# A cross-attention block in split fp32r: x in three buffers, and work of the first steps and of every fourth step in another order or on another engine

## The reference

```python
scale = HEAD_DIM ** (-0.5)
h = _layernorm(x, gamma, beta)                       # over the last axis of 256
Q = (h @ Wq).reshape(B, NQ, N_HEADS, HEAD_DIM)
K = (context @ Wk).reshape(B, NC, N_HEADS, HEAD_DIM)
V = (context @ Wv).reshape(B, NC, N_HEADS, HEAD_DIM)
attn = jnp.einsum('bihd,bjhd->bhij', Q, K)
attn = jax.nn.softmax(attn, axis=-1) * scale
vals = jnp.einsum('bhij,bjhd->bihd', attn, V).reshape(B, NQ, INNER)
out = vals @ Wo + bo
return x + out
```

## Time and profile before

| | us |
|---|---|
| runs | 339.98 (median), 339.65, 396.95 |
| the profiled execution | 339.38 |
| its span | 337.3 |
| mean granted TensorE clock | 0.995 of full speed |

### The profile page before, as it was taken

How to read it: one execution, slowest core, us unless ns; L and a number is a source line. 1 busy time by engine, 2 the same in 40 slices (tenths; PEclk the granted TensorE clock), 3 DMA queues, 4 the chain that set the end, 5 groups by cost and what they waited for, 6 DMA issues and landing times.

```text
span 337.3 us, 9748 instructions
## 1 busy us (share of the span) xinstructions
PE 322.7 (96%) x3773; PEld 283.2 (84%) x3773; DVE 258.4 (77%) x585; ACT 254.7 (76%) x799; POOL 161.3 (48%) x294
## 2 busy tenths in 40 slices
PE   5999997999999999999999999999999999999986
PEld 4868777888889988888998888899888889988864
DVE  4898855787887788787877878877887878668764
ACT  4898883888778877787677887778777876777872
POOL 4688954463563364631563435633646315333330
PEclk9999997999999999999999999999999999999999
DMA  6860001020000200002000200002000010001000
GB/s 182 258 186 2 1 26 32 2 82 7 2 3 2 87 0 3 2 2 87 1 3 2 81 10 2 0 3 88 2 2 0 2 34 2 2 0 34 2 3 31
DMA packets 10764, 10.70 MB, mean 32 GB/s; under 512 B 960, under 2 KB 10176, under 8 KB 10720
## 3 DMA queue, kind: packets, MB, share of 16 engines
q1 hardware_dynamic: 10192, 9.64, 9.3%
q10 hardware_dynamic: 416, 0.33, 0.3%
q0 software_dynamic: 112, 0.13, 0.2%
HBM read 8.00 MB, written 2.10 MB: 30 GB/s over the span
## 4 chain that ended last, share of the span: by engine, by line
PE 78%; ACT 9%; DVE 6%; POOL 4%; issue 1%; DMA 1%; DVEq 0%; SPq 0%; POOLq 0%; ACTq 0%
PE mix_ps L866 15%; PE ring_ps L837 12%; PE ring_ps L932 11%; PE o_ps L957 10%; PE ring_ps L890 9%; PE ring_ps L989 8%; PE ring_ps L1023 6%; ACT prob L475 4%; DVE prob L689 2%; PE ring_ps L1030 2%; ACT qk_hi L485 2%; PE ring_ps L910 1%; PE o_ps L798 1%; POOL prob L383 1%; POOL wo_lo L322 1%
## 5 line engine op out<-in xcount | busy, mean ns | idle before, releaser
L383 POOL TENSOR_SCALAR prob<-prob,inv 128x256 f32<-128x256 f32 x192 | 90.3, 488 | 121.7 <-DVE inv L681 121.7
L475 ACT ACTIVATE prob<-ring_ps,neg_max 128x256 f32<-128x256 f32 x256 | 118.3, 474 | 21.7 <-DVE neg_max L674 21.7
L674 DVE TENSOR_REDUCE neg_max<-ring_ps 128x2 f32<-128x512 f32 x128 | 81.3, 677 | 1.0 <-PE ring_ps L837 0.8
L866 PE MATMUL mix_ps<-prob_t,v_sb 128*64 128x256 f32 x504 | 61.5, 385 | 0.5 <-DVE prob_t L779 0.5
L779 DVE COPY prob_t<-ring_ps 128x512 f32<-128x512 f32 x64 | 41.9, 687 | 21.6 <-PE ring_ps L989 20.3
L699 DVE TENSOR_TENSOR qk_lo<-ring_ps,qk_hi 128x512 fp32r<-128x512 f32 x64 | 44.1, 689 | 15.6 <-ACT qk_hi L485 15.6
L475 ACT ACTIVATION_READ_ACCUMULATOR prob<-ring_ps,neg_max 128x1 f32 x256 | 52.8, 206 | 0.0
L485 ACT ACTIVATE qk_hi<-ring_ps 128x512 fp32r<-128x512 f32 x64 | 38.7, 605 | 14.1 <-PE ring_ps L932 14.1
L866 PEld LDWEIGHTS mix_ps<-prob_t,v_sb 128*64 128x64 f32 x504 | 33.4, 136 | 18.3 <-issue 0.6
L989 PE MATMUL ring_ps<-ident,prob 64*128 64x64 f32 x1024 | 38.6, 223 | 1.8 <-DVE prob L689 1.1
L837 PE MATMUL ring_ps<-qk_hi 64*128 64x256 f32 x256 | 39.9, 301 | 0.3 <-DVE qk_lo L699 0.3
(11 more groups left out here) (116 smaller groups left out, 697.0 us busy)
## 6 DMA issues: line engine op xcount, KB each, us to landing
x_in<-in_x_dram SPq DMA_DIRECT2D x8, 256.0 KB, 2.9
out_dram<-y_sb SPq DMA_DIRECT2D x7, 256.0 KB, 2.2
c_in<-in_ctx_dram SPq DMA_DIRECT2D x7, 192.0 KB, 2.8
w_raw<-in_L_xattn_Wq_dram SPq DMA_DIRECT2D x8, 128.0 KB, 3.4
w_raw<-in_L_xattn_Wo_dram SPq DMA_DIRECT2D x4, 256.0 KB, 6.3
w_raw<-in_L_xattn_Wk_dram SPq DMA_DIRECT2D x4, 128.0 KB, 3.8
w_raw<-in_L_xattn_Wk_dram SPq DMA_DIRECT2D x8, 64.0 KB, 3.5
w_raw<-in_L_xattn_Wv_dram SPq DMA_DIRECT2D x2, 256.0 KB, 5.1
```

The costliest lines, as they stand in the source:

```text
L383: last = nc.gpsimd.tensor_scalar(prob[:, e, r, :], prob[:, e, r, :], inv[:, e, r:r + 1], SCALE, ALU.mult, ALU.mult)
L475: last = nc.scalar.activation(prob[:, e, r, :], score_bank(u, e)[:, r * ROWS:(r + 1) * ROWS], ACT.Exp, bias=neg_max[:, e, r:r + 1], accum_ ...
L674: nc.vector.tensor_reduce(neg_max[:, e, :], score_bank(u, e)[:, :].rearrange("p (r j) -> p r j", r=RT), AX, ALU.max, negate=True).then_inc ...
L866: last = nc.tensor.matmul(ps[h * HALF:(h + 1) * HALF, first:first + ROWS], v_sb[:, w // RT % 2, j, p * P + h * HALF:p * P + (h + 1) * HALF ...
```

## The change

- x_in has three buffers. x of sequence 2 is loaded with no wait, x of sequence b >= 3 after x_norm and x_bias of sequence b-3. SyncE's loop is written out step by step, and the load of bo moves from GpSimd's queue to the end of SyncE's weight loads.
- `bias(0)` moves from the end of step 2 to the end of step 4, ahead of `bias(1)`.
- Sequence 1's norm moves from GpSimd to VectorE, in step 1, one row tile on either side of `keys_lo(0)`. Its statistics move from the end of step 0 to places further up in step 0.
- The low part of weight piece 8 moves from VectorE (step 0) to GpSimd, ahead of step 0. GpSimd's `context_for_values(0)` goes: V of sequence 0 is made from c_t itself.
- h's high part moves from between `keys_lo(0)` and `keys_lo(1)` to behind `last_head` in the steps 2, 6, ..., 26. In step 2 weight pieces 20 and 21 stay ahead of `keys_lo(1)`.
- The first step's banks are taken in the same order as in all others, so that the second pair's scores of step 1 wait for one copy of each engine in place of two.

```diff
@@ the lists, buffers and banks
-    LO_VECTOR = (0, 4, 5, 8, 9, 13, 20, 21)
-    LO_POOL = (1, 2, 3, 6, 7, 10, 11, 12, 14, 15, 16, 17, 18, 19, 22, 23)
+    LO_VECTOR = (0, 4, 5, 9, 13, 20, 21)
+    LO_POOL = (1, 2, 3, 6, 7, 8, 10, 11, 12, 14, 15, 16, 17, 18, 19, 22, 23)
...
-        x_in = sb("x_in", [P, 2, RT, D])
+        x_in = sb("x_in", [P, X_BUFS, RT, D])
...
-            return ring[u % 3]
+            return ring[u % 3 if u else 2]
...
-            return ring[(u - (e // 2 if u else 1 - e // 2)) % 3][e % 2]
+            return ring[(u - e // 2) % 3][e % 2]
...
-        x_banks = ring[2]
+        x_banks = ring[0]
@@ SyncE
+            sp.dma_start(bo_b[:, :], b_o.partition_broadcast(P)).then_inc(bo_in, 16)
...
                 b = of_seq(u, LOAD, 2)
                 if b is not None:
-                    sequence, used = number(b + turns(2)), number(b - 1 + turns(2))
-
-                    sp.wait_ge(x_norm_ready, used)
-                    sp.wait_ge(x_bias_ready, used)
-                    load_x(b, sequence)
-                    sp.wait_ge(c_turned, used)
-                    load_c(b, sequence)
+                    if b >= X_BUFS:
+
+                        sp.wait_ge(x_norm_ready, b - X_BUFS + 1)
+                        sp.wait_ge(x_bias_ready, b - X_BUFS + 1)
+                    load_x(b)
+
+                    sp.wait_ge(c_turned, b - 1)
+                    load_c(b)
@@ GpSimd
             for n in (1, 2, 3, 6, 7):
                 weight_lo(n)
-            pool.dma_start(bo_b[:, :], b_o.partition_broadcast(P)).then_inc(bo_in, 16)
-            context_for_values(0)
+            weight_lo(8)
...
                     deviation(b)
-                    norm(b)
+                    if b >= 2:
+                        norm(b)
...
                 if u == 2:
                     weight_lo(22)
-                    pool.wait_ge(bo_in, 16)
-                    bias(0)
...
+                for b in (0, 1) if u == PER_SEQ else (of_seq(u, SPLIT_H, 2),):
+                    if b is not None:
+                        if b == 0:
+
+                            pool.wait_ge(bo_in, 16)
...
+                        pool.wait_ge(x_norm_ready, b + 1)
+                        bias(b)
@@ VectorE
                 if u == 0:
-                    weight_lo(8)
                     weight_lo(9)
+                    rows_statistics(1, 0)
...
+                if u == 1:
+
+                    dve.wait_ge(x_turned, 1)
+                    norm(1, (0,))
                 keys_lo(0)
+                if u == 0:
+                    rows_statistics(1, 1)
+                if u == 1:
+                    norm(1, (1,))
+                if u == 2:
+                    weight_lo(20)
+                    weight_lo(21)
...
                 if u < 2:
                     last_head()
+                keys_lo(1)
+                if u == 0:
+                    variance(1)
+                if measured is not None:
+                    deviation_base(measured)
+                if u >= 2:
+                    last_head()
                 b = of_seq(u, SPLIT_H, 1)
                 if b is not None:
...
                         nc.vector.tensor_copy(h_hi[:, b % 2, d, :], h_full[:, d, :])\
                             .then_inc(h_hi_ready, 1)
-                if u == 2:
-                    weight_lo(20)
-                    weight_lo(21)
-                keys_lo(1)
-                if measured is not None:
-                    deviation_base(measured)
-                if u >= 2:
-                    last_head()
...
-                        statistics(1)
+                        deviation_base(1)
                         weight_lo(13)
@@ TensorE
-                            pe.wait_ge(prob_t_ready[h], BATCH * (u - 1) + (2 if u == 1 else 1))
+                            pe.wait_ge(prob_t_ready[h], BATCH * (u - 1) + 1)
...
-                pe.wait_ge(c_val_ready, b + 1)
+
+                tiles = c_val if b else c_t
+                if b:
+                    pe.wait_ge(c_val_ready, b)
```

More of the change, by code:

```diff
@@ L33, in cross_attention_block @@
     STEPS = SEQS * PER_SEQ
-    LOOP_STEPS, LOOPS = 2 * PER_SEQ, 3
     LAST = STEPS + 2
@@ L61, in cross_attention_block @@
     FOR_O = {0: 15, 1: 20, 2: 23, 3: 24}
-    LO_VECTOR = (0, 4, 5, 8, 9, 13, 20, 21)
-    LO_POOL = (1, 2, 3, 6, 7, 10, 11, 12, 14, 15, 16, 17, 18, 19, 22, 23)
+    LO_VECTOR = (0, 4, 5, 9, 13, 20, 21)
+    LO_POOL = (1, 2, 3, 6, 7, 8, 10, 11, 12, 14, 15, 16, 17, 18, 19, 22, 23)
     WARM = 6
+    X_BUFS = 3
     SHIFT = 16
@@ L159, in cross_attention_block @@
         w_in = [sem(f"w_in{i}") for i in range(len(PIECES))]
-        x_loaded = [sem("x_loaded0"), sem("x_loaded1")]
+        x_loaded = [sem(f"x_loaded{k}") for k in range(X_BUFS)]
         c_loaded = [sem("c_loaded0"), sem("c_loaded1")]
@@ L212, in of_seq @@
             return b if rest == 0 and first <= b < SEQS else None
[L214 to L224, removed]
         def before(n, pieces):
@@ L242, in _ @@
         def _(sp):
-            def number(n):
-                return n if isinstance(n, int) else sp.snap(n)
             def load_weight(n):
@@ L264, in load_weight, with load_x, load_c, step @@
                                  rows.rearrange("(g p) n -> p g n", p=P)).then_inc(w_in[n], 16)
[L266 to L272, removed]
+            def load_x(b):
+                sp.dma_start(x_in[:, b % X_BUFS, :, :], x_v[b]).then_inc(x_loaded[b % X_BUFS], 16)
+            def load_c(b):
+                sp.dma_start(c_in[:, b % 2, :, :], c_v[b]).then_inc(c_loaded[b % 2], 16)
+            load_x(0)
             for n in range(0, 10):
                 load_weight(n)
-            load_x(1, 1)
-            load_c(1, 1)
+            load_x(1)
+            load_c(1)
             for n in range(10, len(PIECES)):
                 load_weight(n)
-            def step(u, turns):
+            sp.dma_start(bo_b[:, :], b_o.partition_broadcast(P)).then_inc(bo_in, 16)
+            def step(u):
                 b = of_seq(u, LOAD, 2)
                 if b is not None:
-                    sequence, used = number(b + turns(2)), number(b - 1 + turns(2))
-                    sp.wait_ge(x_norm_ready, used)
-                    sp.wait_ge(x_bias_ready, used)
-                    load_x(b, sequence)
-                    sp.wait_ge(c_turned, used)
-                    load_c(b, sequence)
+                    if b >= X_BUFS:
[4 more added lines that the diff above has]
+                    load_c(b)
                 b = of_seq(u, PUT)
@@ L296, in step @@
                 elif b is not None:
[L297 to L301, removed]
+                    sp.wait_ge(y_ready, b + 1)
+                    sp.dma_start(y_v[b], y_sb[:, b % 2, :, :]).then_inc(y_free[b % 2], 16)
+            for u in range(-1, LAST):
+                step(u)
             sp.wait_ge(y_free[0], 16 * (SEQS // 2 + 1))
@@ L335, in norm @@
                 for r in range(RT):
-                    last = nc.gpsimd.tensor_scalar(x_norm[:, r, :], x_in[:, b % 2, r, :],
+                    last = nc.gpsimd.tensor_scalar(x_norm[:, r, :], x_in[:, b % X_BUFS, r, :],
                                                    mean_var[:, r, 0:1], rstd[:, r:r + 1],
@@ L341, in context_for_values @@
             def context_for_values(b):
-                if b >= 2:
+                if b >= 3:
                     pool.wait_ge(v_made, PER_SEQ * (b - 1))
@@ L351, in bias @@
                 for r in range(RT):
-                    last = nc.gpsimd.tensor_tensor(x_bias[:, b % 2, r, :], x_in[:, b % 2, r, :],
+                    last = nc.gpsimd.tensor_tensor(x_bias[:, b % 2, r, :], x_in[:, b % X_BUFS, r, :],
                                                    bo_b[:, :], ALU.add)
@@ L396, in step @@
                     context_for_values(b)
-                b = of_seq(u, SPLIT_H, 1)
                 if u == 2:
                     weight_lo(22)
-                    pool.wait_ge(bo_in, 16)
-                    bias(0)
[L404 to L411, removed]
+                for b in (0, 1) if u == PER_SEQ else (of_seq(u, SPLIT_H, 2),):
+                    if b is not None:
+                        if b == 0:
+                            pool.wait_ge(bo_in, 16)
+                        if b >= 2:
+                            pool.wait_ge(y_ready, b - 1)
+                        pool.wait_ge(x_norm_ready, b + 1)
+                        bias(b)
             for u in range(-1, LAST):
-                step(u, lambda n: 0)
+                step(u)
         @block.scalar
@@ L597, in rows_statistics @@
             def rows_statistics(b, r):
-                k = b % 2
-                dve.wait_ge(x_loaded[k], 16 * (b // 2 + 1))
+                k = b % X_BUFS
+                dve.wait_ge(x_loaded[k], 16 * (b // X_BUFS + 1))
                 nc.vector.bn_stats(bn[:, r, :], x_in[:, k, r, :]).then_inc(stats_done, 1)
@@ L618, in statistics, with norm @@
                 deviation_base(b)
-            def norm(b):
```

(14 more changed lines are left out.)

## The result

The changed kernel takes 331.77 us, the median of four runs (331.59 to 332.07); the kernel before took 339.81 beside it. One of the four runs of the kernel before took 396.95 us and is left out of the ratio, which is 0.9767, 95% interval 0.9748 to 0.9786: faster by 2.3%. The forecast was 331.9 us. The profiled execution takes 332.07 us, 7.3 less than the profiled one before; its span is 330.1 us, 7.2 less.

A forecast was written before the change was run, and what follows sets the result against it. TensorE, busy for 322.7 of 337.3 us, bounds the kernel, so gains lie in its idle time and clock. 0.6 + 0.49 + 4.33 + 2.4 = 7.8 us off 339.38 gives 331.6, median about 331.9; range 329.8 to 335.2.

The forecast's parts named there:

- Part 1, the load of x: Step 3: sequence 2's x loads early, so VectorE's and TensorE's stalls and the low clock go; 4.33 us, bounds 2.6 to 4.43.
- Part 2, h's high part: Steps 6, 10, ..., 26: fourth head's scaling takes 0.62 us for 1.34 with GpSimd quiet; 0.40 us each, 2.4 in all.
- Part 3, steps 0 to 2: First steps: 0.6 us gained by step 2's start (bounds 0 and 1.05), and 0.49 us in step 2.
- the prediction's own sign: Start of step 2: its scores by 31.2 us in place of 31.8 if the forecast is right.
- step 0's gain would not be lost ahead of step 1's maxima: Step 1: as the statistics leave the place ahead of the maxima, step 0's gain of some 0.4 us is kept.
- the lower bound: End of step 1: turn's second half at 30.5 if norm waits for GpSimd's scalings and the fourth head for a low part.
- its alternative, a sum 0.3 us smaller: Step 1: by the skill's rule, the norm on VectorE contends with GpSimd's scaling, making the sum 0.3 us smaller.
- The norm rival: Steps 0 to 2: norm on VectorE and GpSimd's scalings block each other; nothing gained or up to 0.5 lost; chance 0.10.
- L1011 waited for nothing: Sign of a right forecast: L1011 with no wait for wv_lo.
- rivals on the fourth head: Steps 6, 10, ..., 26: the fourth head stays late; 2.4 us back, 334.3 us; chance 0.15.
- on the clock after the change: Step 3 keeps a wait or the clock still falls; price 1.7 us, 333.6 us; chance 0.12.
- on placement: All 32 steps: third buffer moves prob and others by 2,048 bytes a partition, slower access; 346 at 0.45 us a step; chance 0.03.

The follow-up runs named there:

- x_three_only: Kernel before with x in three buffers and nothing else, the load of bo and the bias staying where they were: 335.02 us, ratio 0.9881.
- low_part_waits_only: Kernel before, h's high part unmoved, but GpSimd's low part of h waits until VectorE has scaled the fourth head (steps 6, 10, ..., 26): 336.59 us.
- norm_on_gpsimd: Changed kernel with sequence 1's norm back on GpSimd, ahead of step 1's scaling: 331.50 us.
- step1_head_alone: Changed kernel, but in step 1 GpSimd starts low parts of pieces 15 to 18 only after VectorE scales the fourth head: 330.89 us, 330.62 us run again.

## Why the prediction was right, point by point

**Part 1, the load of x.** Forecast 4.33 us from step 3, measured 4.2 by the windows and 4.4 in the times of x_three_only alone (339.44 - 335.02). The cause was shown by that run. The clock's share was seen as fixed; it is a matter of the execution, 0 or some 1.7 us of the 4.3. Since 13 of 18 runs of the kernel before had it, the forecast from one profiled execution met the median; with one of the other five the same reading would have given 2.9 us (an estimate: step 3's 12.55 us in low_part_waits_only less 9.61). That is luck.

**Part 2, h's high part.** Forecast 0.40 us in each of six steps, 2.4 in all; measured 0.38 in the first, and 2.3 over the six. That the gain comes from GpSimd being late and not from VectorE's order was argued; low_part_waits_only showed it. The rule that the prediction took from the Trainium skill (SBUF — State Buffer, section "Who interferes with whom"), that such a VectorE instruction and a GpSimd one lock each other out for whole instructions, agrees: 1.34 and 0.62 us in step 6, and 1.39 and 0.61 us in step 1, for the same two instructions.

**Part 3, steps 0 to 2.** This is the term that was mis-sized: 1.09 us forecast (0.6 by step 2's start and 0.49 in step 2), 0.67 measured by the start of step 3. The 0.6 came to 0: the scores of step 2 start at 31.82 for 31.77, where the prediction's own sign asked for 31.2. It is a sum of two. Step 0 gave 0.61, more than the 0.4 forecast; step 1, which was to give 0.2, took 0.66 back.

Two steps of the reasoning failed. The first is that step 0's gain would not be lost ahead of step 1's maxima, as the statistics had left that place. The low part of piece 13 still stood there and waited 0.81 us for ScalarE, which was no earlier, and 0.19 us of the gain was left at the maxima. norm_on_gpsimd, with the norm where it was before, shows the same: its steps 0 and 1 together take 19.01 us (12.26 to 31.27) for 19.21 before (12.56 to 31.77), 0.2 us less. The second is the collision at the end of the step. The prediction had it as the lower bound ("the fourth head for a weight's low part") and took a value between, when the same overlap stood as the main finding in part 2; its alternative, a sum 0.3 us smaller, was the nearer one. GpSimd freed by 2.4 us ran into its next queued work, and that work ran beside VectorE's scaling. With this one collision taken away, step 2's scores start at 31.09 in step1_head_alone, 0.68 us earlier than before: the forecast's 0.6, by a wait that the change did not have.

The norm rival (0.10) was right in kind: the norm instructions themselves took 0.59 and 0.42 us, 0.3 more than the 0.73 for both before step 0, and step 1 is 0.3 us shorter with the norm on GpSimd. Most of the harm was done by the low parts. Step 2 gave its 0.49 and a little more (11.27 us for 11.99), and L1011 waited for nothing, as forecast. Which of the edits in steps 0 and 2 gave what is not shown: no run separates them.

**The sum.** 7.8 us forecast, 7.3 by the profiles, 8.0 by the medians. That the median came within 0.2 us of the forecast is partly luck: the 0.4 us missing from steps 0 to 2 and 0.1 each from steps 3 and 4 don't show in it, as the profiled execution was the slowest of its four after the change, while the one before was on the quick side of its kernel's times. The rivals on the fourth head, on the clock after the change and on placement did not come about. The lower end of the range, 329.8, is not quite its own sum, as 339.38 - 8.4 - 1 is 330.0; nothing hangs on it.

## What to carry to other kernels

When work leaves a queue, ask what that engine does with the freed time: here GpSimd's next instructions moved up beside VectorE's critical one and took the gain back, and a wait that kept the helper idle for 0.95 us was worth 0.75 us in that step. When a stage starts earlier, ask which engines' work ahead of it did not get shorter: here ScalarE's high part came no earlier, and 0.4 of step 0's 0.6 us ended there. When a critical instruction takes twice its usual time, as the scaling did here, look at the other engine's timeline at that moment before touching the order on its own. And a stall of TensorE may cost more than its length in some executions and not in others, so look at several times before a clock's fall is counted as a fixed price.

## What the runs showed of the hardware that had not been expected

Behind a stall of TensorE of 2.6 us the granted clock fell in some executions of one kernel and not in others (13 of 18 runs at a mean of 0.994 or 0.995, 5 at 0.999 or 1.000). Where it fell, it did so at the start of the 12 products or among them (2.90 or 2.41 us), and step 3 took 13.94 or 14.13 us, for 12.55 where it did not. With stalls of 0.68 and 1.70 us it fell in none of eight runs.

In the changed kernel TensorE is some 4% slower for a while at a granted clock of 1.00: the 12 products take 1.41 and 1.42 us in steps 3 and 4 and 1.37 from step 5 on. These are its chain's rows:

```profile
49.38 1.41 PE o_ps L954 x12
...
59.05 1.42 PE o_ps L954 x12
...
69.07 1.37 PE o_ps L954 x12
```

norm_on_gpsimd has 1.41 in step 3, while x_three_only and step1_head_alone have 1.36, and their step 3 takes 9.60 and 9.58 us for 9.76. The slower pace accounts for step 4's 10.09 us against 9.97 and most of step 3's 0.15 us over the forecast; what sets it off stays open, and no run was made for it.
